# Row sums of a 4096x4096 matrix: eight one-column matmuls, or blocks turned on VectorE and one matmul of 32 columns

## The reference, cut to what matters

```python
def _cxin_conv(x, a, eps, W, b):                 # twice: (x, adj, W1) and (x2, adj, W2)
    ax = a @ x                                   # [4096,4096] @ [4096,128]
    h = ax + (1.0 + eps[0]) * ax
    for i in range(3):
        h = relu(h @ W[i].T + b[i])
    return h

def gcn(X, A, W, b):
    A_hat = A + eye(4096)
    deg = sum(A_hat, axis=1)                     # the row sums this document is about
    d = where(deg > 0, rsqrt(deg), 0.0)
    return (d[:, None] * A_hat * d[None, :]) @ X @ W.T + b

x = layernorm(x + concat(conv(x, W1), conv(x2, W2)) @ Wm.T + bm)
x = layernorm(x + gcn(x, adj, W, b))
```

## Time and profile before

| | |
|---|---|
| median of 3 runs | 618.41 us (618.28 to 618.61) |
| the profiled execution's own time | 619.22 us |
| its span, first to last instruction | 617.4 us |
| mean granted TensorE clock | 0.995 of full speed |
| TensorE busy | 596.5 us, 97% |
| VectorE busy | 536.8 us, 87% |
| ScalarE busy | 368.1 us, 60% |

### The profile page before, as it was taken

How to read it: one execution, slowest core, us unless ns; L and a number is a source line. 1 busy time by engine, 2 the same in 40 slices (tenths; PEclk the granted TensorE clock), 3 DMA queues, 4 the chain that set the end, 5 groups by cost and what they waited for, 6 DMA issues and landing times.

```text
span 617.4 us, 8024 instructions
## 1 busy us (share of the span) xinstructions
PE 596.5 (97%) x2692; PEld 485.0 (79%) x2692; DVE 536.8 (87%) x680; ACT 368.1 (60%) x443; POOL 26.3 (4%) x21
## 2 busy tenths in 40 slices
PE   4999999999999999999999999999989999999994
PEld 3888888888888888888888888868768778778873
DVE  5999989987987995988899899955898988998994
ACT  5545346842445772354676255584877797797781
POOL 0000000001100000200000110000200000000011
PEclk9999999999999999999999999999999999999997
DMA  8967555433555433455543476583779999999800
GB/s 292 409 230 288 196 205 198 163 115 132 205 204 188 157 132 136 154 192 197 204 141 131 162 289 244 188 341 136 287 299 346 331 378 389 341 371 394 335 35 35
DMA packets 21288, 141.55 MB, mean 229 GB/s; under 512 B 2320, under 2 KB 2832, under 8 KB 5008
## 3 DMA queue, kind: packets, MB, share of 16 engines
q1 hardware_dynamic: 20544, 139.15, 60.7%
q10 hardware_dynamic: 720, 2.10, 0.9%
HBM read 139.14 MB, written 2.10 MB: 229 GB/s over the span
## 4 chain that ended last, share of the span: by engine, by line
PE 85%; DVE 10%; ACT 2%; issue 1%; DMA 1%; POOL 1%; POOLq 0%; SPq 0%; DVEq 0%; ACTq 0%
PE ps L332 74%; DVE alo L625 7%; PE pd L350 6%; PE pd L362 2%; PE pd L358 1%; PE pd L394 1%; ACT ahi L478 1%; DMA raw<-a_t 1%; DVE stats L681 1%; DVE z L770 1%; POOL rstd L865 1%; ACT outn L508 1%; PE ps L407 0%; DVE mv L689 0%; DVE raw L760 0%
## 5 line engine op out<-in xcount | busy, mean ns | idle before, releaser
L478 ACT ACTIVATE ahi<-raw 128x1024 fp32r<-128x1024 f32 x255 | 267.8, 1059 | 217.5 <-PE ps L332 213.4
L625 DVE TENSOR_TENSOR alo<-raw,ahi 128x1024 fp32r<-128x1024 f32 x255 | 307.6, 1218 | 52.9 <-ACT ahi L478 51.7
L332 PE MATMUL ps<-ahi,x1hi 128*128 128x512 f32 x504 | 162.7, 399 | 12.0 <-DVE alo L619 8.2
L332 PE MATMUL ps<-ahi,x2s 128*128 128x512 f32 x512 | 159.9, 391 | 0.0
L332 PE MATMUL ps<-alo,x1hi 128*128 128x512 f32 x504 | 158.5, 391 | 0.0
L332 PE MATMUL ps<-ahi,x1lo 128*128 128x512 f32 x504 | 158.3, 390 | 0.0
L332 PEld LDWEIGHTS ps<-ahi,x1hi 128*128 128x128 f32 x504 | 92.4, 189 | 40.6 <-issue 13.5
L332 PEld LDWEIGHTS ps<-ahi,x2s 128*128 128x128 f32 x512 | 96.7, 189 | 20.2
L332 PEld LDWEIGHTS ps<-ahi,x1lo 128*128 128x128 f32 x504 | 94.9, 188 | 20.2
L332 PEld LDWEIGHTS ps<-alo,x1hi 128*128 128x128 f32 x504 | 94.9, 188 | 19.9
L332 PE MATMUL ps<-alo,x2s 128*128 128x512 f32 x256 | 80.6, 391 | 0.0
(11 more groups left out here) (59 smaller groups left out, 265.2 us busy)
## 6 DMA issues: line engine op xcount, KB each, us to landing
raw<-a_t SPq DMA_DIRECT2D x124, 1024.0 KB, 4.8
raw<-a_t SPq DMA_DIRECT2D x7, 512.0 KB, 8.8
xn<-x SPq DMA_DIRECT2D x3, 1024.0 KB, 8.3
out<-outn ACTq DMA_DIRECT2D x3, 512.0 KB, 4.5
par<-params SPq DMA_DIRECT2D x1, 708.0 KB, 14.2
xn<-x SPq DMA_DIRECT2D x2, 256.0 KB, 4.6
raw<-a_t SPq DMA_DIRECT2D x2, 256.0 KB, 5.2
xn<-x SPq DMA_DIRECT2D x1, 512.0 KB, 8.3
```

What stands on the lines that cost most here:

```text
L332: mm = pe.matmul(ps[bank][:, :], block_of(w, n), a[c], start=(n == 0 and k == 0), stop=(n == JB - 1 and k == 2))
L478: act.activation(ahi[:, n % SPLIT, :], raw_tile(layer, n), ACT.Copy).then_inc(hi_ready, 1)
L625: dve.tensor_tensor(alo[:, n % SPLIT, :], raw_tile(layer, n), as_f32(ahi[:, n % SPLIT, :]), ALU.subtract).then_inc(lo_ready, 1)
```

## The change

The partition sum is made in another way. At step 5 of plan 0 (4 of plan 1) VectorE transposes `rowsum_all` within its 32 x 32 blocks into `turned`; one step later it adds each run of 32 columns, which leaves `partial`, 128 x 32: partition 32g + i, column b holds the sum over the 32 partitions of group g for row 32b + i. TensorE's `merge` waits for it on a new semaphore and does one matmul with `same_place` (128 x 128, one where two partitions have the same place within their group of 32) as weights and `partial` as 32 moving columns; so every partition gets the total of each row of its place, in `totals`, 128 x 32 in PSUM. In `degrees` VectorE multiplies by the mask `my_group`, which keeps the columns that belong to the partition's own group, and adds each run of four columns: `degree`, 128 x 8, now in SBUF, in the same layout as before. GpSimd writes the two new constants at the start, and the wait for the constants in TensorE's and VectorE's programs stands behind the first quarter instead of at the very start.

```diff
+TB = 32
+GROUPS = P // TB
+DVE_TURN = (5, 4)
...
             def merge(q):
                 wait(pe, h_ready, q * (4 * M) + 4 * M)
-                for k in range(KB):
-                    pe.matmul(degree[:, k:k + 1], rowsum_all[:, k * P:(k + 1) * P], ones[:, :],
-                              start=(k == 0), stop=(k == KB - 1), skip_group_check=True)
+                wait(pe, partial_ready, q + 1)
+                pe.matmul(totals, same_place[:, :], partial[:, :], start=True, stop=True, skip_group_check=True)
...
-            pe.wait_ge(const_ready, 3)
             layer0_quarter(0, None)
+            pe.wait_ge(const_ready, 2 + GROUPS)
...
+            def turn_rowsums(q):
+                wait(dve, raw_used, q * PAIRS + PAIRS)
+                dve.transpose(turned[:, :], rowsum_all[:, :]).then_inc(turned_ready, 1)
+
+            def add_turned(q):
+                wait(dve, turned_ready, q + 1)
+                dve.tensor_reduce(partial[:, :], turned[:, :].rearrange("p (b r) -> p b r", r=TB),
+                                  mybir.AxisListType.X, ALU.add).then_inc(partial_ready, 1)
+
             def degrees(q):
-                dve.tensor_scalar(degc[:, :], degree, 1.0, TINY, ALU.add, ALU.max).then_inc(deg_ready, 1)
-                dve.tensor_scalar(degpos[:, :], degree, 1.0, 0.0, ALU.add, ALU.is_gt).then_inc(deg_ready, 1)
+                dve.tensor_tensor(own[:, :], totals, my_group[:, :], ALU.mult).then_inc(own_ready, 1)
+                wait(dve, own_ready, q + 1)
+                dve.tensor_reduce(degree[:, :], own[:, :].rearrange("p (k g) -> p k g", g=GROUPS),
+                                  mybir.AxisListType.X, ALU.add).then_inc(degree_ready, 1)
+                wait(dve, degree_ready, q + 1)
+                dve.tensor_scalar(degc[:, :], degree[:, :], 1.0, TINY, ALU.add, ALU.max).then_inc(deg_ready, 1)
+                dve.tensor_scalar(degpos[:, :], degree[:, :], 1.0, 0.0, ALU.add, ALU.is_gt).then_inc(deg_ready, 1)
...
+                if n == DVE_TURN[plan]:
+                    turn_rowsums(q)
+                if n == DVE_TURN[plan] + 1:
+                    add_turned(q)
...
-            pool.memset(ones[:, :], 1.0).then_inc(const_ready, 1)
+            pool.memset(same_place[:, :], 0.0).then_inc(const_step, 1)
+            pool.memset(my_group[:, :], 0.0).then_inc(const_step, 1)
+            ...                                  # four affine_select and four memset more
```

More of the change, by code:

```diff
@@ L120, in build @@
         rowsum_all = sb("rowsum_all", [P, QW])
+        turned = sb("turned", [P, QW])
+        partial = sb("partial", [P, QW // TB])
+        own = sb("own", [P, QW // TB])
+        degree = sb("degree", [P, KB])
+        my_group = sb("my_group", [P, QW // TB])
+        same_place = sb("same_place", [P, P])
         xb = sb("xb", [P, KB, P])
@@ L126, in build @@
         gain = sb("gain", [P, 2])
-        ones = sb("ones", [P, 1])
         identity = sb("identity", [P, P])
@@ L142, in build @@
         merged = pd[:, 0:2, :].rearrange("p c (k d) -> p (c k) d", d=P)
-        degree = pd[:, 2, 0:KB]
+        totals = pd[:, 2, 0:QW // TB]
         params_in = sem("params_in")
@@ L167, in build @@
         xb_ready = sem("xb_ready")
+        turned_ready = sem("turned_ready")
+        partial_ready = sem("partial_ready")
+        own_ready = sem("own_ready")
+        degree_ready = sem("degree_ready")
         deg_ready = sem("deg_ready")
@@ L818, in layer1_quarter @@
                         add_identity(q, n + AHEAD)
-            dve.wait_ge(const_ready, 3)
             split_x(0)
             layer0_quarter(0, None)
+            dve.wait_ge(const_ready, 2 + GROUPS)
             dve.wait_ge(params_in, 16)
@@ L872, in _ @@
                                base=0, pattern=[[-1, P]], channel_multiplier=1).then_inc(const_ready, 1)
-            pool.wait_ge(const_ready, 3)
+            pool.memset(same_place[:, :], 0.0).then_inc(const_step, 1)
+            pool.memset(my_group[:, :], 0.0).then_inc(const_step, 1)
+            pool.wait_ge(const_step, 3)
+            place = same_place[:, :].rearrange("p (g c) -> p g c", c=TB)
+            for g in range(GROUPS):
+                pool.affine_select(out=place, in_=place, compare_op=ALU.not_equal, fill=1.0, base=-TB * g,
+                                   pattern=[[0, GROUPS], [-1, TB]], channel_multiplier=1).then_inc(const_step, 1)
+                pool.wait_ge(const_step, g + 4)
+            of_group = my_group[:, :].rearrange("p (k g) -> p k g", g=GROUPS)
+            for g in range(GROUPS):
+                pool.memset(of_group[g * TB:(g + 1) * TB, :, g], 1.0).then_inc(const_ready, 1)
+            pool.wait_ge(const_ready, 2 + GROUPS)
             with pool.Fori(0, QUARTERS) as q:
```

## The result

The changed kernel took 613.03 us (median of 4 runs, 612.64 to 613.82) against 618.35 us for the kernel before on the same chip. The ratio is 0.9912, 95% interval 0.9900 to 0.9924: 5.4 us faster by the ratio, where 612.9 us was forecast. Two later comparisons gave ratios of 0.9901 and 0.9902, 6.1 us. The profiled execution took 613.1 us with a span of 611.3 us.

A forecast was written before the change was run, and what follows sets the result against it. TensorE's unbroken chain was taken to bound layer 0, with the path alternating between TensorE and VectorE in layer 1. -5.88 + 0.39 = -5.49 us from 618.41 gave 612.9 us; range 611.8 to 615.8.

The forecast's parts named there:

- What goes: Eight row-sum matmuls before each merge on TensorE: 1.68 us a quarter, all on the path, 6.72 us in four quarters.
- The table's 25 ns: Skill's price per one-column TensorE matmul; by it the change gives back at most some 1.4 us; the forecast used 0.105 us.
- One matmul of 32 columns: New TensorE matmul before each merge: two pairs, 0.21 us, bounds nothing to 0.86 us; saving 1.47 us a quarter.
- Transpose and sum: Two VectorE passes before the merge: 1.135 us each, 2.27 together, costing nothing while under 2.57 us.
- The cover of 2.57 us: Layer 0: time from first `hlo` ending (114.29) to TensorE's dense layer needing it (116.86); additions beyond it cost three quarters.
- The fullest quarter: VectorE's busiest quarter: 97.0 us busy of 99.5, still fits; its 2.8 us lead on the last block loses at most 0.6.
- One sign: Sign of being right in the changed profile: VectorE's `z` must still wait for the merge; no size given.
- The last quarter's gain: Last quarter's merge, layer 1: its 1.47 us saving counts in full, since `z` waited 3.04 us and moves earlier with TensorE.
- Rival A: Last quarter's saving is lost in layer 1; 4.0 us remain, giving 614.4 us; chance 0.08.
- Behind the merge: VectorE's multiplication and sum in `degrees`: 0.39 us, paid once, in layer 1's first quarter; bounds 0.14 to 0.76 us.
- Block 24: Layer 1 block for which TensorE stood 1.60 us; should start some 5.5 us earlier, at about 447.1.
- the sum: Whole kernel: -5.88 us on TensorE plus 0.39 us on VectorE behind the merge, -5.49 us in all.

## Why the prediction was right, point by point

**What goes.** 1.68 us a quarter from the chain, all on the path: shown by leaving them out and by issuing eight again. The prediction held that nothing hides beneath them; left out, they are worth 1.79 us a quarter, so its 1.68 was 0.11 too small.

**The table's 25 ns against the row's 0.105 us.** The rule of the Trainium skill ("VectorE: DVE Perf Modes", TRN2 errata) would have made the gain an estimated 1.4 us at most. The changed kernel gained 5.4, and 16 pairs cost 1.71 us with 32 columns as they did 1.68 with one. For float32 matmuls, each with a weight load of its own, the row on this kernel was the right price. That it is the weight load which sets it was argued and not shown.

**One matmul of 32 columns.** Forecast 0.21 us, 0.14 in the chain: within the bounds. Against a merge with no small matmuls in front of it (3.57 us) the two pairs cost 3.79 - 3.57 = 0.22 us, so the price was right. What was mis-sized is the difference: 5.36 - 3.79 = 1.57 us a quarter, where 1.47 was forecast.

**Transpose and sum.** Forecast 1.135 us of VectorE's time each, 2.27 together; the `hlo` moved by 2.24. Here the trace agrees with the Trainium skill ("Vector Engine (DVE) Microarchitecture Reference", the reshape front-end): 1.237 us for 1024 columns is the duration of other single passes (1.217 us for `alo`), also for 4-byte elements. The cover of 2.57 us was right within about 0.05 us, as the two kernels with extra transposes show.

**The fullest quarter.** Three lines of the changed kernel:

```profile
338.38 1.23 DVE L673 TENSOR_TENSOR z<-pd,xb 128x1024 f32<-128x1024 f32 x1
389.00 1.21 DVE L636 TENSOR_TENSOR alo<-raw,ahi 128x1024 fp32r<-128x1024 f32 x1
392.63 0.39 PE L344 MATMUL ps<-ahi,x1hi 128*128 128x512 f32 x1
```

VectorE's part of the last block of layer 0 ends at 390.21 and TensorE starts on it at 392.63: 2.4 us of lead, where 2.8 less at most 0.6 was expected. One sign failed: I had written that `z` must still wait for the merge. In this quarter it does not any more; it starts at 338.38, right behind its merge's end at 338.34, so nothing was lost, but there is no slack left in that place either.

**The last quarter's gain.** Rival A gave it a chance of being lost in layer 1. The kernel without the eight matmuls shows 1.78 us between the last two merges, in full; in the changed kernel this piece shrank by 1.45.

**Behind the merge.** Forecast 0.39 us once. The two new links and their gaps take 0.11 + 0.02 + 0.20 + 0.02 = 0.35 us, and `degc` 0.17 where it had 0.07, since it now waits too. Together 0.45, and 0.5 us between the marks. I had left out the wait in front of `degc`.

**Block 24.** It was to start at 447.1 and starts at 446.44, 6.1 us earlier than before and not 5.5; TensorE waits 1.57 us for it, where it was 1.60.

```profile
446.44 0.73 PE L344 MATMUL ps<-ahi,x1hi 128*128 128x512 f32 x2 [1.57 <-DVE x1lo L775]
```

**What was not in the sum.** The forecast was 5.49 us, the spans differ by 6.1. Missing were 4 x 0.10 = 0.40 us in the price of what goes, and nine dense layers at 0.04 us, 0.36 us, through the new allocation. Against that stand 0.11 us more behind the merge than forecast, and 0.12 us in the last quarter, where the piece between the last two merges shrank by 1.45 and not by 1.57; the unused tiles alone cost 0.07 of these, the rest is open. That makes 5.49 + 0.40 + 0.36 - 0.11 - 0.12 = 6.0 us.

**How much of the hit is luck.** The mechanism came out as forecast. That the median fell within 0.1 us of the forecast (613.03 and 612.9) is luck: the terms left out are worth 0.5 to 0.6 us, and the same kernel measured 612.21 and 612.72 us later.

## What to carry to other kernels

A row of tiny float32 matmuls costs its pairs of weight load and matmul, here 0.11 us each from 1 to 128 columns: count the pairs in the chain, not the columns. Before work is moved to an engine that is 90% busy, look for the first instruction behind the place of insertion for which another engine waits: the distance to its use is the cover, here 2.57 us of which 0.27 were left, and an average busy share says nothing of it. A result that is ready before its companion is best consumed while the engine still waits for that companion.

## What the runs showed of the hardware that was not expected

Moving tiles by some 5 KB in each partition of SBUF changed the time of 12 matmuls from 2.79 to 2.75 us, in each of nine places and in every kernel with the new layout that kept them free of waits. Of their operands only `whi` and `wlo` are allocated behind the new tiles; `h`, `hhi` and `hlo` stayed where they were. The dense layers of the last quarter, in float32 and with `par`, which moved too, stayed at 3.43 us. What about an address matters was not tried.

The first quarter, whose instructions are the same in all of these kernels but for a wait at the start, ended between 107.75 and 109.15 us (start of the first dense layer). The difference arises early: from 12 to 16 us, where the DMA engines are busy all the time, TensorE does 15 matmuls in the changed kernel's first profile and 20 in the one that ended this quarter first. Behind it the distances between merges repeat to 0.01 us in three executions of the changed kernel, and the time behind the last merge to 0.07. For effects below 1 us the marks are the better measure.
